# Attention statistics by DMA instead of by TensorE, and three of four score steps seeded by ScalarE

## The reference, cut to what matters

```python
xn = group_norm(x, gn_gamma, gn_beta)
qkv = jnp.einsum('bchw,oc->bohw', xn, w_qkv).reshape(B, 3, nh, d, H * W)
q, k, v = (qkv[:, 0], qkv[:, 1], qkv[:, 2])
scores = jnp.einsum('bhci,bhcj->bhij', q, k) * d ** (-0.5)
attn = jax.nn.softmax(scores, axis=-1)
out = jnp.einsum('bhij,bhcj->bhci', attn, v).reshape(B, C, H, W)
proj = jnp.einsum('bchw,oc->bohw', out, w_proj) + b_proj[None, :, None, None]
return xn + proj
```

## Time and profile before

| | us |
|---|---|
| median of three runs | 5492.59 (5486.8 to 5498.76) |
| the profiled execution's own time | 5486.11 |
| its span, first to last instruction | 5484.3 |
| TensorE busy | 4957.6 (90%) |
| VectorE busy | 3959.3 (72%) |
| GpSimd busy | 2966.1 (54%) |
| ScalarE busy | 2793.4 (51%) |

### The profile page before, as it was taken

The page is one execution under the profiler, slowest core; times in us unless marked ns, Lnnn a source line. Parts: engine busy times, 40 slices in busy tenths (PEclk is TensorE's granted clock), DMA queues, the critical chain, the costliest instruction groups (busy, mean ns, idle before and its releaser), DMA issues. The chain is left out here.

```text
span 5484.3 us, 73719 instructions
## 1 busy us (share of the span) xinstructions
PE 4957.6 (90%) x22320; PEld 2313.6 (42%) x22320; DVE 3959.3 (72%) x6354; ACT 2793.4 (51%) x4750; POOL 2966.1 (54%) x2339
## 2 busy tenths in 40 slices
PE   7999999999899999999978869969978996999788
PEld 3333333333333333333346657745544553554344
DVE  4788888883588888888333334458887886898898
ACT  2666666664266666666411111135544554555455
POOL 0555555555055555555437757746645664665675
PEclk9999999999999999999978879989999998999899
DMA  2000000000000000000134435569969998998998
GB/s 73 1 1 1 1 1 1 1 1 34 30 1 1 1 1 1 1 1 1 37 87 128 128 111 163 162 242 365 388 268 350 371 389 304 378 387 350 396 410 358
DMA packets 320271, 812.24 MB, mean 148 GB/s; under 512 B 70094, under 2 KB 137556, under 8 KB 319758
## 3 DMA queue, kind: packets, MB, share of 16 engines
q0 software_dynamic: 193536, 679.59, 32.8%
q1 hardware_dynamic: 126478, 129.39, 6.9%
HBM read 708.40 MB, written 100.43 MB: 147 GB/s over the span
## 5 line engine op out<-in xcount | busy, mean ns | idle before, releaser
L653 POOL TENSOR_TENSOR arena<-arena 128x1024 f32<-128x1024 f32 x480 | 1168.0, 2433 | 955.2 <-ACT arena L1310 952.6
L1841 DVE TENSOR_REDUCE arena<-ps 128x2 f32<-128x1024 f32 x1024 | 1252.2, 1223 | 457.5 <-PE ps L805 454.2
L705 POOL DMA_INDIRECT arena<-corners,arena x1152 | 1094.2, 950 | 687.6 <-issue 301.6
L1310 ACT ACTIVATE arena<-ps 128x1024 f32<-128x1024 f32 x1024 | 995.4, 1022 | 611.2 <-PE ps L834 609.4
L2065 DVE SCALAR_TENSOR_TENSOR ps<-arena,ps 128x256 f32<-128x256 f32 x2304 | 956.3, 483 | 230.9 <-DVEq L2059 220.9
L1172 PE MATMUL ps<-arena 128*128 128x512 f32 x2304 | 1047.5, 598 | 0.2
L834 PE MATMUL ps<-arena 64*128 64x512 f32 x4096 | 977.9, 590 | 19.0 <-ACT ps L1293 19.0
L847 PE MATMUL ps<-arena 128*64 128x512 f32 x4096 | 991.3, 605 | 0.0
L1503 ACT ACTIVATE ps<-arena 128x256 f32<-128x256 f32 x1152 | 500.2, 469 | 471.0 <-DMA arena<-corners,arena 208.4
L689 POOL DMA_INDIRECT arena<-corners,arena x576 | 544.8, 946 | 275.5 <-issue 244.3
L1860 DVE TENSOR_TENSOR arena<-arena 128x1024 f32<-128x1024 f32 x480 | 630.5, 1314 | 79.3 <-ACT arena L1310 79.3
(11 more groups left out here) (165 smaller groups left out, 4108.5 us busy)
## 6 DMA issues: line engine op xcount, KB each, us to landing
corners<-arena SPq DMA_DIRECT2D x256, 256.0 KB
arena<-corners,arena POOLq DMA_INDIRECT x1728, 7.7
img<-in_x SPq DMA_DIRECT2D x8, 1024.0 KB, 9.3
corners<-arena SPq DMA_DIRECT2D x128, 64.0 KB, 2.2
arena<-in_wd SPq DMA_DIRECT2D x2, 2304.0 KB, 8.5
between<-img SPq DMA_DIRECT2D x4, 1024.0 KB, 5.9
arena<-between SPq DMA_DIRECT2D x4, 1024.0 KB, 10.5
resid<-img SPq DMA_DIRECT2D x8, 512.0 KB, 3.4
```

The costliest lines, as they stand in the source:

```text
L653: pool.tensor_tensor(SUMS[u % 2][:, 0], SUMS[u % 2][:, 0], PAIR[g % 2][:, :, 0], ALU.add).then_inc(sum_a, 2)
L705: pool.indirect_dma_start(G3[4 * k + t].rearrange("p a c -> p (a c)"), None, table256[b], bass.IndirectOffsetOnAxis(ap=IS3[:, k, t:t + 1], ...
L1310: af(P[n % 4].rearrange("p h q -> p (h q)"), ps[:, 2 * (n % 2):2 * (n % 2) + 2, :].rearrange("p h q -> p (h q)"), ACT.Exp, scale=float(D) ...
L1841: v.tensor_reduce(mxp[i % 2][:, :, j], ps[:, 4:6, :], AX.X, ALU.max).then_inc(mx_done, 1)
```

## The change

**Maxima.** `max_rows`, `row_copy`, `wide_rows` and `wide_copy` are gone, and with them `MSTAT`, `MROW` and the order `aux_at`. VectorE writes the eighth step's maxima to `MNEG` and, scaled and in 16 bits, to `MROWS` (128 partitions x 2 heads). The SyncE queue sends each of the four pieces of a block to a row in DRAM (`send_row`), and once all four have landed one DMA reads that row for all 128 partitions into `MWIDE` (`spread_rows`). `MWIDE` is now double, and has the two heads interleaved, so readers take every second 16-bit element.

**Sums.** GpSimd adds the two halves of the sums in pair 0 of the next block (`fold`, two instructions of 128x512), and `row_sums` has half the matmuls. One row of each head's sums goes to DRAM, comes back as 128 partitions x 2 x 4 (`SINV`), is inverted in one instruction on VectorE in pair 6, goes to DRAM again and is read for 64 partitions per head into `RC` (`send_sums`, `spread_inverses`). The last block of an image keeps its old way.

**Seeds.** ScalarE seeds every step that is not a multiple of four (from step 2 on), where it seeded the odd ones. TensorE seeds only every fourth step and step 1.

```diff
-        MROW = [att.f32(CHUNK, dt=F16) for _ in range(2)]
         ORAW = att.f32(CHUNK)
         RC = att.f32(CHUNK)
-        MWIDE = att.f32(2, CHUNK, dt=F16)
-        MSTAT = att.f32(128)
+        MWIDE = [att.f32(CHUNK, 2, dt=F16) for _ in range(2)]
+        MNEG = att.f32(2)
+        MROWS = [att.f32(4, 2, dt=F16) for _ in range(2)]
+        SINV = att.f32(2, 4)
         COEF = att.f32(128, dt=F16)
...
-        def wide_in(g):
-            return g // (NT // 2) + 1 if g % (NT // 2) == NT // 2 - 1 and g // (NT // 2) + 1 < BLOCKS else None
-
-        def seeds_in(g):
-            return 2 * g + 3 if 2 * g + 3 < STEPS else None
-
-        aux = [what for what in opening if what[0] == "rows"] + [("wide0", 0), ("wide1", 0)]
-        for g in range(STEPS // 2):
-            if rows_in(g) is not None:
-        aux.append(("rows", rows_in(g)))
-            if wide_in(g) is not None:
-        aux += [("wide0", wide_in(g)), ("wide1", wide_in(g))]
-            if sums_in(g) is not None:
-        aux.append(("sums", sums_in(g)))
-        aux.append(("sums", BLOCKS - 1))
-        aux_at = {what: k for k, what in enumerate(aux)}
-        assert len(aux) == 7 * BLOCKS
+        def is_seeded(n):
+            return n >= 2 and n % 4 != 0
+
...
+        def send_row(u, t):
+
+            sp.wait_ge(mrow_ready, 4 * u + t + 1)
+            if u >= 2:
+                sp.wait_ge(wide_ready, 16 * (u - 1))
+            sp.dma_start(row_buf[u % 2, t * 256:(t + 1) * 256].rearrange("(p h) -> p h", h=2),
+                         MROWS[u % 2][:, t, :]).then_inc(row_sent, 16)
+
+        def spread_rows(u):
+
+            sp.wait_ge(row_sent, 64 * (u + 1))
+            if u >= 2:
+                sp.wait_ge(p_ready, NT * (u - 1))
+            sp.dma_start(MWIDE[u % 2].rearrange("p q h -> p (q h)"),
+                         row_buf[u % 2, :].partition_broadcast(128)).then_inc(wide_ready, 16)
+
+        def send_sums(u):
+
+            sp.wait_ge(sums_copied, u + 1)
+            for h in range(2):
+                sp.dma_start(sum_buf[h:h + 1, :], RC[64 * h:64 * h + 1, :]).then_inc(sums_sent, 16)
+            sp.wait_ge(sums_sent, 32 * (u + 1))
+            sp.dma_start(SINV, sum_buf.rearrange("h (p i) -> p h i", p=128)).then_inc(sums_back, 16)
+
+        def spread_inverses(u):
+
+            sp.wait_ge(rc_done, u + 1)
+            if u >= 1:
+                sp.wait_ge(rc_wide, 32 * u)
+            sp.dma_start(inv_buf.rearrange("h (p i) -> p h i", p=128), SINV).then_inc(inv_sent, 16)
+            sp.wait_ge(inv_sent, 16 * (u + 1))
+            for h in range(2):
+                sp.dma_start(RC[64 * h:64 * h + 64, :],
+                             inv_buf[h, :].partition_broadcast(64)).then_inc(rc_wide, 16)
+
+        for u in range(BLOCKS + 1):
+            if u < BLOCKS:
+                send_row(u, 0)
+            if u >= 2:
+                send_sums(u - 2)
+            if u < BLOCKS:
+                send_row(u, 1)
+            if u >= 2:
+                spread_inverses(u - 2)
+            if u < BLOCKS:
+                send_row(u, 2)
+                send_row(u, 3)
+                spread_rows(u)
+
         sp.wait_ge(mx_done, STEPS)
         with sp.Fori(0, NCH // 2) as n2:
             for p in range(2):
...
         def normalized(u):
-            pool.wait_ge(rc_done, 8 * (u + 1))
+            if u < BLOCKS - 1:
+                pool.wait_ge(rc_wide, 32 * (u + 1))
+            else:
+                pool.wait_ge(rc_done, BLOCKS + 7)
             pool.wait_ge(o_done, u + 1)
             pool.tensor_tensor(QF[u // QB][:, (u % QB) * CHUNK:(u % QB + 1) * CHUNK], ORAW, RC,
                                ALU.mult).then_inc(at_done, 1)
+
+        def fold(u):
+
+            pool.wait_ge(sum_a, NT * (u + 1))
+            pool.wait_ge(sum_b, NT * (u + 1))
+            for h in range(2):
+                to = SUMS[u % 2][:, h]
+                pool.tensor_tensor(to[:, 0], to[:, 0], to[:, 1], ALU.add).then_inc(folded, 1)
         cast_queries(0)
         cast_queries(1)
         for g in range(STEPS // 2):
             u, pair = g // (NT // 2), g % (NT // 2)
             if pair == 0 and u >= 2:
-                pool.wait_ge(aux_ready, aux_at[("sums", u - 2)] + 1)
+                pool.wait_ge(sums_ready, u - 1)
             if pair == 0 and u == 1 and b == 0:
                 pool.wait_ge(borders, 16 * BORDER_WRITES)
             pool.wait_ge(p_ready, 2 * g + 2)
...
+            if pair == 0 and u >= 1:
+                fold(u - 1)
             if pair == 4 and u + 2 < BLOCKS:
                 cast_queries(u + 2)
             if pair == 12 and u >= 1:
                 normalized(u - 1)
+        fold(BLOCKS - 1)
         normalized(BLOCKS - 1)
         pool.drain().then_inc(arrived, 1)
...
-        def max_rows(i):
-
-            k = aux_at[("rows", i)]
-            pe.wait_ge(mstat_ready, i + 1)
-            if k >= 1:
-                pe.wait_ge(aux_done, k)
-            tr(ps[:, 7, 0:128], MSTAT, ident_s[:, :]).then_inc(aux_ready, 1)
-
         def scores(n):
             u, kc = n // NT, n % NT
             if kc == 0:
-                pe.wait_ge(aux_done, aux_at[("rows", 4 * u + 3)] + 1)
+                pe.wait_ge(wide_ready, 16 * (u + 1))
             if n >= 2:
                 pe.wait_ge(p_ready, n - 1)
-            if n % 2 == 0 or n == 1:
+            if is_seeded(n):
+                pe.wait_ge(seeded, seeds_before[n] + 1)
+            else:
                 for h in range(2):
                     rows = slice(64 * h, 64 * h + 64)
-                    mm(ps[:, 2 * (n % 2) + h, :], COEF[rows, :], MROW[u % 2][rows, :], start=True, stop=False,
+                    mm(ps[:, 2 * (n % 2) + h, :], COEF[rows, :], MWIDE[u % 2][rows, :, h], start=True, stop=False,
                        tile_position=(64 * h, 0))
-            else:
-                pe.wait_ge(seeded, n // 2)
             for h in range(2):
                 rows = slice(64 * h, 64 * h + 64)
                 last = mm(ps[:, 2 * (n % 2) + h, :], KF[u // QB][rows, kc * 128:(kc + 1) * 128],
                           QF[u // QB][rows, (u % QB) * CHUNK:(u % QB + 1) * CHUNK], start=False, stop=True,
-                          tile_position=(64 * h, 0), skip_group_check=n % 2 == 1 and n > 1)
+                          tile_position=(64 * h, 0), skip_group_check=is_seeded(n))
             last.then_inc(st_scores, 1)
         def values(n):
...
         def row_sums(u):
-            pe.wait_ge(sum_a, NT * (u + 1))
-            pe.wait_ge(sum_b, NT * (u + 1))
-            pe.wait_ge(aux_done, aux_at[("sums", u)])
-            for part in range(2):
-                for h in range(2):
-                    last = mm(ps[64 * h:64 * h + 64, 7, :], ONES, SUMS[u % 2][:, h, part, :], start=(part == 0),
-                              stop=(part == 1), tile_position=(0, 64 * h))
-            last.then_inc(aux_ready, 1)
-
-        def wide_rows(u, h):
-
-            k = aux_at[(f"wide{h}", u)]
-            pe.wait_ge(aux_done, k)
-            rows = slice(64 * h, 64 * h + 64)
-            mm(ps[:, 7, :], COEF[rows, :], MROW[u % 2][rows, :], start=True, stop=True,
-               tile_position=(64 * h, 0)).then_inc(aux_ready, 1)
+            pe.wait_ge(folded, 2 * (u + 1))
+            if u >= 1:
+                pe.wait_ge(sums_copied, u)
+            for h in range(2):
+                last = mm(ps[64 * h:64 * h + 64, 7, :], ONES, SUMS[u % 2][:, h, 0, :], start=True, stop=True,
+                          tile_position=(0, 64 * h))
+            last.then_inc(sums_ready, 1)
         for i in first:
             unit(i)
         for what, i in opening:
             if what == "unit":
                 unit(i)
-            elif what == "max":
+            else:
                 leading_scores(i)
-            else:
-                max_rows(i)
-        for h in range(2):
...
-        def row_copy(i):
-
-            act.wait_ge(aux_ready, aux_at[("rows", i)] + 1)
-            af(MROW[i // 4 % 2][:, i % 4 * 128:(i % 4 + 1) * 128], ps[:, 7, 0:128], ACT.Copy,
-               scale=1.0 / (HALF_SCALE ** 2 * ROW_COEF)).then_inc(aux_done, 1)
-
-        def wide_copy(u, h):
-
-            act.wait_ge(aux_ready, aux_at[(f"wide{h}", u)] + 1)
-            af(MWIDE[:, h, :], ps[:, 7, :], ACT.Copy, scale=1.0 / ROW_COEF).then_inc(aux_done, 1)
-
         def seed(n):
-            act.wait_ge(aux_done, aux_at[("wide1", n // NT)] + 1)
+            act.wait_ge(wide_ready, 16 * (n // NT + 1))
             act.wait_ge(p_ready, n - 1)
-            af(ps[:, 2:4, :].rearrange("p h q -> p (h q)"), MWIDE.rearrange("p h q -> p (h q)"), ACT.Copy,
-               scale=ROW_COEF).then_inc(seeded, 1)
+            bank = 2 * (n % 2)
+            af(ps[:, bank:bank + 2, :], MWIDE[n // NT % 2].rearrange("p q h -> p h q"), ACT.Copy, scale=ROW_COEF).then_inc(seeded, 1)
         def sums_copy(u):
-            act.wait_ge(aux_ready, aux_at[("sums", u)] + 1)
+            act.wait_ge(sums_ready, u + 1)
             if u >= 1:
```

(95 more changed lines are left out.)

24 lines of the change are left out of this document (17 added, 7 removed).

## The result

| | us |
|---|---|
| before, median of 4 runs | 5489.69 (5485.01 to 5498.76) |
| after, median of 4 runs | 5619.72 (5615.28 to 5631.12) |
| ratio, 95% interval | 1.0238 (1.0217 to 1.0259) |
| after, the profiled execution and its span | 5615.28 and 5613.5 |

A forecast was written before the change was run, and what follows sets the result against it. TensorE was taken to bound the steady pairs. The terms 26 - 8 + 16 + 20 + 19 - 16 - 2 - 2 + 2 gave 55 us off per image, 110 for both: 5380 us, range 5335 to 5465.

The forecast's parts named there:

- DMA chains: Between a block's last maxima and the first scores needing them: write and broadcast read take 6.3 to 7.0 us of 8.5, hidden.
- sign of being wrong in kind: Two steady pairs take more than 8.67 us, or the first scores of a block wait for a DMA.
- The broadcast comes late: Rival at block boundaries: 12 us instead of 7, each waits 3.5, time 5485, no change; chance 0.07.
- Maxima out of TensorE: Transpositions 16 us and block boundaries 20 us off per image; VectorE gets one tiny instruction per eighth maximum in idle time.
- Fewer seed matmuls: In each two pairs with lead scores, one of two seed matmul groups goes: 26 us off per image.
- two seeds in a row: After an even pair ScalarE seeds both next steps, overlapping; the second step's scores wait 0.07 us: 8 us on per image.
- neither rival about them: ScalarE's seeds longer, 5620 at 0.5 us more, chance 0.08; or ScalarE does not overlap the seeds, 5463, chance 0.10.
- the half-rate read of TensorE: Rival: TensorE reads the interleaved row at half rate, one group in two pairs costs 0.22 us more, 5432; chance 0.04.
- Row sums: Pair with the row sums: half the matmuls, and the wait for the copy of the maxima goes: 19 us off per image.
- Locks between GpSimd and VectorE: GpSimd's folds and shorter pairs around its other instructions delay VectorE: 1.1 us per block, 16 us on per image.

The follow-up runs named there:

- the gather: Kernel after, with each piece of maxima first gathered into one row in SBUF, then sent to DRAM as one row of 512 bytes: 5419.53 us, ratio 0.9874.
- the last kernel: Kernel after, with the maxima gathered in SBUF before they go to DRAM and their scaling on ScalarE instead of VectorE: 5384.85 us, ratio 0.9806.
- lead 40: Kernel after with lead scores 40 steps ahead instead of 36: 5439.94 us; with the scaling of the maxima on ScalarE too, 5396.29 us.

## Why the prediction was wrong

I compare one block, between two lead scores that follow row sums. It takes 74.78 us before (601.48 to 676.26), 78.65 after (624.06 to 702.71), 71.74 with the gather (582.86 to 654.60), and 70.87 with the scaling on ScalarE too (578.30 to 649.16). The rows that end the waits in the block of the kernel after:

```profile
656.84 0.39 PE L868 MATMUL ps<-arena 64*128 64x512 f16 x2 [0.41 <-DVE arena L1857]
...
686.35 0.61 PE L885 MATMUL ps<-arena 64*128 64x512 f16 x2 [4.59 <-DMA arena<-row_buf]
686.75 3.62 PE L889 MATMUL ps<-arena 64*128 64x512 f32 x8
...
699.66 0.39 PE L868 MATMUL ps<-arena 64*128 64x512 f16 x2 [0.48 <-DVE arena L1857]
```

Between 78.65 and 70.87 lie 7.78 us: 4.59 of waiting for the broadcast, 2.03 net in the pairs behind it, the first of which runs at the lower clock, 0.89 of lead scores that wait for VectorE (0.41 and 0.48), and 0.27 of other shifts. Over 30 blocks that is 233 us, and the two kernels differ by 235.

- **DMA chains: the step that failed.** It said that two transfers of 6.3 to 7.0 us fit into 8.5, "hidden". The slack was nearly right, 8.0. The transfers took 12.2; with the gather they take 6.4, and are hidden. The row of 3.5 us that priced the write has as many bytes, but goes from SBUF to SBUF (`bnf1`, 64 pieces of 8 bytes), not as pieces of 4 bytes side by side into DRAM. The prediction's own sign of being wrong in kind, first scores of a block that wait for a DMA, came at all 15 boundaries of the first image. It had the right rival, **The broadcast comes late**, even with the 12 us and the small pieces of 4 bytes, but gave it 0.07 and 5485. Its price left out the clock: after waits of 4.2 and 4.6 us TensorE came back at 1.2 GHz, and a boundary costs 6.6 us (4.59 + 2.03) instead of 3.5. The prediction itself said that the trace has no such transfer; the range should have followed that, and not the nearest rows alone.
- **Maxima out of TensorE: right on TensorE, wrong on VectorE.** The extra time of the boundary is gone in the last kernel: the two pairs around it take 8.60 (630.85 to 639.45), where they took 9.98. The transpositions are gone too. But "one tiny instruction per eighth maximum, in its idle time" became 1.39 us in the median. The step counted VectorE's free time and did not ask whether GpSimd was at work then, though the same prediction told of the lock two steps further on. Taking it away brought 50 us in the kernel after (about 15 of them a shorter wait for the broadcast), 44 at lead 40 and 35 with the gather, so it costs 35 to 44 us over both images. The section that the prediction cited from the Trainium skill ("SBUF — State Buffer", section Who interferes with whom) tells the two instructions apart: a `tensor_scalar` can use the port pair that GpSimd shares, if its operands allow it, and a `tensor_reduce` on this chip never does. The trace agrees, with 1.67 for the scaling and 0.17 for the reduce ahead of it, under one add.
- **Fewer seed matmuls and two seeds in a row: half right.** ScalarE does overlap the seeds (two are listed as 1.98 us, each 1.03 long), and neither rival about them came. Nor did the half-rate read of TensorE: its seeds from the interleaved row take 0.23 (582.65 to 582.88). The budget of the Trainium skill ("ScalarE: Activation LUTs", Rules for kernel authors), by which the prediction worked out 1.15 us, is given there for an instruction whose bias is one value per partition; the seeds have no such bias. But two steady pairs take 8.61 (582.42 to 591.03 in the last kernel) and not 8.52: the scores of the pair that waits for the second seed are listed as 2.02 long instead of 1.88, a delay of 0.14 where 0.07 was forecast. This is a size, not the mechanism.
- **Row sums: right.** The pair with them takes 5.20 (643.96 to 649.16), so 0.87 beside a pair of 4.33, with 0.90 forecast.
- **Locks between GpSimd and VectorE: overstated for the folds.** In that block three lead scores wait, 0.86, 0.16 and 0.18, against 0.78 before: 0.42 more, not 1.1. That the sum comes out so closely is luck: this error and that of the seeds cancel (0.68 x 15 = 10 us against 0.09 x 119 = 11). The pair with `normalized` waited before as well. VectorE's add there was stretched by 1.11 us (2.33 - 1.22), and not by "the whole 1.27".
- **The sum.** Forecast 55 us per image; the last kernel gives (5490.43 - 5384.85) / 2 = 52.8. With the two failed terms taken away, by a third transfer and by ScalarE, the time is within 5 us of the forecast; part of that closeness is the luck just named. What is not settled is why the broadcast is quicker behind a row written whole.

## What to carry over

A transfer that the trace does not show is to be priced by its pieces and where they lie, not by its bytes: if the chain has slack 8 and might take 12, move its issue a pair earlier or measure it alone first. A wait of TensorE can cost more than its length (here 6.6 us for 4.6), so a rival with a wait needs the clock in its price. Before giving VectorE a tiny instruction in its idle time, look at what GpSimd runs at that moment.

## What the runs showed of the hardware

- 128 writes of 4 bytes into DRAM: 7.8 us side by side, 2.7 us with 64 bytes and 2.6 with 512 bytes between their starts; into one SBUF row 2.0. But 256 writes of 16 bytes side by side into DRAM took 1.9.
- The broadcast of a row to 128 partitions took 4.7 us for a quarter of it (64 KB) and for the whole (256 KB), but 3.3 for the whole where the row had been written 512 bytes at a time. Why is open.
- GpSimd's add of 128 x 1024 held a VectorE scaling of 128 x 2 until its own end (1.67 us instead of 0.17), and did not hold a VectorE reduce of 128 x 16 issued in the same add (0.17).
- In a wait of 4.2 us the granted clock of TensorE fell from 1.00. It was 0.50 in the 3.8 us behind the wait, and 0.87 in the mean of the next 4.7.
